# An adaptive-norm FFN with two routed experts on one core: the last two operand splits of an expert block moved to its head, and the gathers of the next block's rows given earlier marks

## What is computed

```python
ys = cond * 512 ** -0.5
d = rsqrt(einsum('bi,io->bo', ys * ys, weight * weight) + 1e-8)
xf = einsum('bsi,io->bso', x * ys[:, None, :], weight) * d[:, None, :]   # 4096 x 512
top1 = argmax(softmax(xf @ gate_w.T))                                    # 0 or 1
masked = xf[None] * one_hot(top1).T[:, :, None]
h = relu(einsum('end,edh->enh', masked, w1) + b1[:, None, :])
routing = (einsum('enh,ehd->end', h, w2) + b2[:, None, :]).sum(axis=0)
shared = relu(xf @ sw1 + sb1) @ sw2 + sb2
return x + routing + shared
```

## Time and profile before

| what | value |
|---|---|
| time, 3 executions | 1387.49, 1388.06 (median), 1388.64 us |
| the profiled execution | 1387.0 us, span 1385.2 us |
| PE busy, matmuls | 1362.6 us (98%), 5990 |
| DVE, ACT, POOL busy | 996.0 (72%), 673.1 (49%), 365.5 us (26%) |
| mean granted clock of PE | 0.994 |

### The profile page before, as it was taken

One profiled execution on the slowest core, in us unless ns is written; L12 is line 12 of the kernel. 1 busy time (PEld: TensorE's weight loads), 2 busy tenths in 40 slices (PEclk: granted clock), 3 DMA queues, 4 the chain that ended last, 5 costly groups with the idle time before them and its releaser, 6 DMA issues.

```text
span 1385.2 us, 17363 instructions
## 1 busy us (share of the span) xinstructions
PE 1362.6 (98%) x5990; PEld 1123.9 (81%) x5990; DVE 996.0 (72%) x1417; ACT 673.1 (49%) x981; POOL 365.5 (26%) x328
## 2 busy tenths in 40 slices
PE   9999999999989999899999999999999999999997
PEld 8888888888878778787888888888888888888886
DVE  7978977768589877857458787868798867833331
ACT  4456644545446554566567444444565455322220
POOL 0000005544555626062000000000000103078786
PEclk9999999999999999999999999999999999999999
DMA  6967586686967678664477897978887789999963
GB/s 203 301 240 207 190 251 208 233 239 218 302 235 255 224 251 271 220 210 164 176 239 249 255 292 249 275 264 257 288 254 232 243 286 309 301 227 262 244 166 49
DMA packets 241337, 330.35 MB, mean 238 GB/s; under 512 B 71696, under 2 KB 106512, under 8 KB 240976
## 3 DMA queue, kind: packets, MB, share of 16 engines
q1 hardware_dynamic: 214480, 295.38, 64.8%
q0 software_dynamic: 21248, 30.30, 10.2%
q10 hardware_dynamic: 5520, 3.54, 0.8%
HBM read 197.06 MB, written 149.29 MB: 250 GB/s over the span
## 4 chain that ended last, share of the span: by engine, by line
PE 94%; DVE 3%; DMA 1%; issue 1%; ACT 0%; POOL 0%; POOLq 0%; DVEq 0%; ACTq 0%
PE bank L2036 40%; PE bank L2114 33%; PE bank L2169 13%; PE bank L1964 6%; DMA rows<-xf_scratch,quad_tab 1%; DVE vb L1510 1%; PE bank L2055 1%; DVE xw L1446 0%; DVE rows L1441 0%; DVE rows L1404 0%; DVE rows L1407 0%; PE bank L1941 0%; PE bank L1947 0%; PE bank L2186 0%; DVE vb L1504 0%
## 5 line engine op out<-in xcount | busy, mean ns | idle before, releaser
L2036 PE MATMUL bank<-xw,w_hi 128*128 128x512 f32 x1792 | 556.4, 392 | 13.3 <-DVE vb L1510 11.3
L2114 PE MATMUL bank<-hl,w_hi 128*128 128x512 f32 x1344 | 414.2, 389 | 0.0
L2036 PEld LDWEIGHTS bank<-xw,w_hi 128*128 128x128 f32 x1792 | 338.4, 189 | 86.1 <-DVE vb L1510 12.9
L1037 ACT CAST hl<-hin 128x512 fp32r<-128x512 f32 x400 | 244.7, 621 | 321.5 <-PE bank L2114 187.8
L1477 DVE TENSOR_TENSOR hl<-hin,hl 128x512 fp32r<-128x512 f32 x400 | 265.2, 686 | 185.6 <-ACT hl L1037 173.8
L2036 PE MATMUL bank<-xw,w_lo 128*128 128x512 f32 x896 | 350.6, 391 | 0.0
L2114 PEld LDWEIGHTS bank<-hl,w_hi 128*128 128x128 f32 x1344 | 252.0, 188 | 53.5 <-DVE hl L1477 0.8
L2114 PE MATMUL bank<-hl,w_lo 128*128 128x512 f32 x672 | 261.4, 389 | 0.0
L2036 PEld LDWEIGHTS bank<-xw,w_lo 128*128 128x128 f32 x896 | 169.3, 189 | 35.6
L1061 ACT ACTIVATE vb<-bank,b 128x512 f32<-128x512 f32 x192 | 130.3, 688 | 116.5 <-PE bank L2036 96.4
L882 POOL DMA_INDIRECT rows<-xf_scratch,quad_tab x128 | 130.3, 1018 | 148.6 <-PE bank L2036 105.3
(11 more groups left out here) (199 smaller groups left out, 1307.1 us busy)
## 6 DMA issues: line engine op xcount, KB each, us to landing
hin<-hidden_scratch SPq DMA_DIRECT2D x168, 512.0 KB
hidden_scratch<-vb SPq DMA_DIRECT2D x120, 512.0 KB
hidden_scratch<-vt SPq DMA_DIRECT2D x48, 512.0 KB
hin<-expert_hidden SPq DMA_DIRECT2D x32, 512.0 KB
w_new<-w_shared SPq DMA_DIRECT2D x52, 256.0 KB, 5.4
expert_hidden<-vb SPq DMA_DIRECT2D x24, 512.0 KB
ring<-x_cols SPq DMA_DIRECT2D x32, 256.0 KB
xf_scratch<-xo SPq DMA_DIRECT2D x32, 256.0 KB, 4.8
```

Source lines behind the costliest of these rows:

```text
L1037: nc.scalar.copy(hl[:, n % HL, 0, :], hin[:, n // 2 % LOADS, n % 2, :]).then_inc(hu_hi, 1)
L2036: last = nc.tensor.matmul(up_bank(u, UP_BANK[c])[p][:], w[:, DOWN_W[c], pair, part], xw[:, c, x, k, :], start=(c in FRESH and n == 1), sto ...
L2114: last = nc.tensor.matmul(bank[p][:], w[:, DOWN_W[c], i, part], hl[:, n % HL, h, :], start=(i == 0 and q == 0), stop=(i == PAIRS - 1 and q ...
```

## The change

Two things. For expert blocks (`s >= BLOCKS`, 4 to 7) the splits of operands 5 and 6 go to the head of the block's first group: on ACT ahead of the takes of product 0 (before, operand 5 was split behind the takes of product 1, and operand 6 behind those of product 2), on DVE ahead of the jobs' sums (before, behind them). In blocks 0 to 3 they stay. And each mark `GATHER_AT[j]` is smaller by 2, for the gathers of all blocks from 4 on: the first is 7 where it was 9, the last 44 where it was 46.

```diff
-GATHER_AT = [9 + 6 * j // 5 for j in range(JW)]
+GATHER_AT = [7 + 6 * j // 5 for j in range(JW)]
@@ block.scalar, up_group
                 wait(act, t3_out[u % 2], DMA * (min(u, GROUPS * FULL) // 2))
                 wait(act, b11_out[u % 2], DMA * (u // 2))
+                if g == 0 and s >= BLOCKS:
+                    block_hi(s, 5)
+                    block_hi(s, 6)
                 take(vb11[u % 2], 0, 0, ACT.Identity)
...
                 take(vb22, 1, 1, ACT.Identity)
-                if g == 0:
+                if g == 0 and s < BLOCKS:
                     block_hi(s, 5)
...
                 if more:
                     block_hi(s + 1, 1)
-                if g == 0:
+                if g == 0 and s < BLOCKS:
                     block_hi(s, 6)
@@ block.vector, up_group
+                if g == 0 and s >= BLOCKS:
+                    block_lo(s, 5)
+                    block_lo(s, 6)
                 for n in jobs:
                     raw_sums(n)
-                if g == 0:
+                if g == 0 and s < BLOCKS:
                     block_lo(s, 5)
...
-                if g == 0:
+                if g == 0 and s < BLOCKS:
                     block_lo(s, 6)
```

## The result

The changed kernel takes 1379.37 us (median of 5 executions, 1378.33 to 1382.0) against 1387.9 us before (median of 5). By the medians that is 8.5 us less. The ratio of the two kernels' times is put at 0.9946, 95% interval 0.9934 to 0.9958, which is 7.5 us, with 5.8 to 9.2 as its bounds. Forecast were 11.4 us. The measured time lies inside the stated range of 1374.5 to 1379.5, by 0.13 us. The profiled execution took 1380.64 us, with a span of 1378.9; it is one of the longer ones.

The account below looks back on a forecast made before the run. PE's matmuls bound the kernel, with stops and slow clock at block turns; gains of 4.0, 3.0, 3.4 and 1.0 us into blocks 4 to 7 sum to 11.4, giving 1376.7 us, range 1374.5 to 1379.5.

Parts of the forecast that it names:

- the signs that the prediction itself gave for being wrong: Clock near 0.5 behind short stops, DMA wait left at flip 3, or ACT-released stop at product 2 of blocks 4 to 6.
- What bounds, and where the gain lies: PE's matmuls bound, 94% of the chain; gain is PE's stops and slow time at turns, set by DVE's late flip 3.
- Marks 2 lower are 2 x 1.36 = 2.7 us earlier; I take the last one at 386.7 to 387.1: Last gather before the turn into block 4, issued at 389.44 before, would go out 2.4 to 2.7 us earlier.
- I take the wait as gone: Flip 3's waits for the last gathers, 3.07, 1.20, 2.45, 1.40 us, vanish; at worst 0.7 us stays at one turn.
- The rival that the transfers land when they did: Bulk stores in the DMA queues set the last rows' landing; only 0 to 2 us won, 1387 us; chance 0.07.
- 2.15 us: Trainium skill's estimate for one 64 KB gather transfer: about 2.0 us plus bytes over 436 GB/s.
- No fall of the clock: Behind PE's shortened stops of 1.4, 1.75 and 1.4 us into blocks 4 to 6, no slow time follows.
- DVE as the next bound, 1.2 us in group 16 and 0.7 in group 24: New PE stops ahead of product 6, awaiting DVE's product 4 addition, take back 1.2 and 0.7 us.
- The cover on ACT: ACT's moved splits precede product 0's takes: room 2.0 us at block 4, 0.4 at block 5; 0.4 lost at block 7.
- The clock falling anyway: Rival: clock falls even after the shorter stops, leaving DVE's own gains of 7.7 us, 1380.4 us; chance 0.18.
- Slower through ACT's splits: Rival: ACT's splits stop PE at product 2 of each expert block's head, 1391 us or above; chance 0.05.

Follow-up runs that it names:

- the repeat: The changed kernel measured once more with nothing changed: 1380.47 us, ratio 0.9952.
- the early marks: Gather marks 7 + j (last 38, not 44): in the changed kernel 1376.02 us; in the kernel before, splits in their old places, 1377.14 us.
- the same reordering on DVE: Flip 2 ahead of operand 0's low split at turns into blocks 4 to 7: with marks 7 + j 1372.15 us; in the changed kernel 1380.04 us.

## Why the prediction was right or wrong

The forecast was 1376.7 us, the measured time 1379.37, within the range by 0.13 us. That it lies inside is in part luck: the medians of the repeat (1380.47) and of the run with the marks alone (1380.39) lie outside. And two of the signs that the prediction itself gave for being wrong came true: DMA waits were left at flip 3 of all four turns, and the granted clock was near 0.5 behind two of the stops (0.57, 0.52).

**What bounds, and where the gain lies**: right. The time came from PE's stops at the turns and the slow clock behind them, released by DVE's third addition, behind the flip that waits for the last gather.

**"Marks 2 lower are 2 x 1.36 = 2.7 us earlier; I take the last one at 386.7 to 387.1"**: too early by 0.4 us. POOL's issue of the gather before took 1.76 us; I had allowed for 1.50. At the turns into blocks 4 to 6 the last gather came 2.0 us earlier against PE, at the turn into block 7 it came 2.5.

**"I take the wait as gone"**: this is the step that failed, and the largest part of the missing time follows from it: 0.94, 0.54, 1.16 and 0.23 us of wait were left. I had worked out myself that with a flight of 5.90 us something of the wait stays at the first turn, and then bet on a shorter flight and let the other turns go by the shift alone. Before, it was 5.9, 4.4, 5.3 and 2.5 us at the four turns (from the issue to the flip's start); after, it is 5.8, 5.8, 6.0 and 4.0. At the first turn it did not shorten, and 2.0 us are less than 3.07; at the others it grew, so that of 2.0, 2.0 and 2.5 us the flip got 0.7, 1.3 and 1.0. The rival that the transfers land when they did was half true. The prediction reckoned that an earlier issue gets ahead of the weight loads. It left out the group's stores, whose place against PE did not move: at the turn into block 5 they are issued from 58.6 us behind the head of block 4 on, before and after, while the gather moved from 63.0 to 61.0. So it went out while the stores were still being issued, where before it came 1 us behind them. The rows of the DMA queues above show that q0's packets came through when the stores were out, and this turn has no loads. That is read from traces; no run moved the stores. At the turn into block 6 the run with the loads a group later puts about 0.8 us on the loads. For the loads at the turn into block 4, and for the difference from one execution to the next, the cause stays open.

The prediction also says that the trace disagrees with 2.15 us "at three of the turns"; its rows show two of them. The third is block 6's, 5.3 us, and at the turn into block 7 the 2.5 us are near it.

**No fall of the clock**: right for stops as short as I had forecast (none behind 1.2 to 1.6 us where the gathers come far earlier, none behind 1.41 us in the repeat), but the stops were 2.3 to 2.5 us, and there the clock fell at some turns. In the profile the turn into block 4 gained 2.7 us instead of 4.0. Into block 5 it was 0.8 instead of 3.0, of which 0.5 is the wait and the rest the clock. Into block 6, without a fall, it was 2.1 instead of 3.4, group 24 counted in, and from the turn into block 7 on about 0.8 instead of 1.0. Together that is 6.4 us in this execution, against 8.5 by the medians.

**DVE as the next bound, 1.2 us in group 16 and 0.7 in group 24**: right. In the runs whose stop into block 4 was the forecast one, PE was idle for 0.92 to 1.03 us in group 16 and came 1.1 to 1.2 us late. In group 24 it was idle for 0.58 and 0.62 us with the early marks, and for 0.62 in the changed kernel. In the changed kernel's first profile group 16 had no stop, since the slow matmuls had made PE late enough.

**The cover on ACT**: right. At product 2 of block 7, where 0.4 us were forecast, about 0.3 us are lost in each profile with the moved splits. Apart from it, 0.43 us of the old stop of 1.42 stand at product 1, where nearly nothing had been forecast.

**The rivals.** The clock falling anyway (1380.4) and the transfers' landing both came true in part, and the result lies between the forecast and the first. Slower through ACT's splits: no stop at product 2 of blocks 4 to 6 was seen.

## What to carry to other kernels

When a wait for a transfer is to be hidden by issuing it earlier, don't take the old flight as an upper bound: ask what else will be in the queues at the new time, and move it by more than the wait; here 5 to 8 us more of lead at the last gather brought the 3 to 4 us that the first step had left. A wait ahead of a chain swallows what is won on the chain: the same reordering on DVE was worth 3.9 us with the rows there in time and nothing without. And a short stop of PE that can't be closed should be pressed below the length at which the clock falls behind it.

## What the runs showed of the hardware

The last gather of a block, 64 KB, took from 2.5 us (turn into block 7, before) to 6.1 us (turn into block 6, the marks alone) from POOL's issue to the release of its reader. Between two profiles of the same kernel it differed by 0.9 us (5.80 and 4.89 at the turn into block 4). In 6 us in which the queue of the stores had 92.5% of the DMA engines' time, that of the gathers had 5.6% (turn into block 5, the changed kernel). POOL's own issue of such a gather took 0.95 us mostly, but 1.75 to 1.76 for the last but one of blocks 4, 5 and 6 in the profiles with the change's marks.

The granted clock fell behind each of PE's stops at these turns that were 2.95 us or longer (before, and the splits alone). Between 2.2 and 2.7 us it fell behind 2.21, 2.26, 2.33, 2.50, 2.56, 2.58 and 2.62 us and not behind 2.23 and 2.54, so there the length alone does not tell. It did not fall behind any of 2.09 us or less (1.23 to 1.76, 1.98, 2.09).
